# Conv-MoE, attention and dense-MoE block on one core: merge, layer norm, q and k moved into the softmax stage, maxima shifted to the dense layer

## The chip, the core and the metric

One NeuronCore of a Trainium2 chip runs the whole program. The metric is the device time of one execution in microseconds (us); lower is better. The five engines are TensorE (PE), VectorE (DVE), ScalarE (ACT), GpSimd (POOL) and SyncE (SP), which here only issues DMAs.

## What is computed

Eight images of 1024 tokens with 96 channels go through a routed layer, attention and a dense layer. The reference, cut:

```python
# 8 images (32x32x96): E = 8 experts, top 2, hidden 384
logits = gn(x) @ Wg + bg;  gates = softmax(where(top2, logits, -inf))
x = x + sum_e gates_e * (gelu(gn(x) @ W1_e + b1_e) @ W2_e + b2_e)      # routed layer
t = ln(x);  q, k, v = split(t @ w_attn.T + b_attn)                     # 6 heads of 16, T = 1024
att = softmax(causal(q @ k.T / 4));  x = x + (att @ v) @ w_proj.T + b_proj
p = topk2(softmax(ln(x) @ gate_w + gate_b)), renormalised              # 4 experts
x = x + sum_e p_e * (gelu(ln(x) @ w1_e + b1_e) @ w2_e + b2_e)          # dense: all 4 are computed
```

## The kernel before

Only two experts of eight are computed in the first layer: the 2048 token copies of an image are sorted by expert into `NBLK` = 23 blocks of 128 rows, with DRAM between (a scatter of x rows to `xs_dram`, a gather of results from `y_dram`). The second layer computes all four experts. float32 accuracy comes from pairs of float16 values: ScalarE writes a high half from PSUM, VectorE then the low half (`low_part`, L1095, and `xs_turn`, L1281), and only the low half frees the bank. Transposes, gate logits and v share one PSUM bank, `ps_m`, in strict turn (`shared()` on each engine); the next user waits for the last one's release.

The order is written out by hand. A loop over `it` from -1 to 10 runs three stages, and each stage is a row of steps (`steps`, L84 on):

- stage a, 28 steps: the routed layer of image `it`, six groups of four blocks, a group in four steps.
- stage s, 26 steps: the scores, exponentials and value products of image `it-1`. Step n has three heads of one 128-key block. PE does the scores of step n and then the values of step n-2; ScalarE takes exponentials in step n. The maxima of the softmax are subtracted by way of two more rows in `qs`, which `maxima` (L1315 on) fills for three heads at a time.
- stage c, 32 steps: the dense layer of image `it-2`, eight groups.

Beside these, tables name chores: (step, chore, unit, offset of the image). `IN_A`, `IN_S`, `IN_C` serve the regular iterations, special tables serve it -1, 0 and 1. Every engine walks the same steps and does its own part of each chore, in order and without looking ahead. So the place in the table is a place in the queue of each engine, not a time: an engine without a wait runs on. On PE the chores of a step come after its scores and values. On VectorE `max` chores come first in a step.

The chores that matter here:

- `max` (72 an image, `MAX_UNITS`): PE puts q·k of 128 queries and up to 512 keys into one of three `ps_r` banks, VectorE reduces it (L1313). In stage s only two banks are free for it. `MAX_C` and `MAX_A` say how many are done in stage c, up to the end of stage a, and then in stage s.
- `gather` (POOL, L646): 16 indirect DMAs, ygot from y_dram. `scatter` 0 to 3 (POOL, L659): four indirect DMAs each, for the next image.
- `merge` (VectorE, L1286 to L1291): waits for the gathers of its half, multiplies with the gates and adds to x. `ln1`: VectorE makes mean and variance (L1122, L1125), POOL the reciprocal deviation (`rstd`, L625 and L627), `ln1_apply` on VectorE waits for it (L1129, L1133). `x1_turn`: PE waits for `xn1_ready`, transposes (L698), ScalarE high half, VectorE low half. `qk`: three matmuls of 512 columns each, for four units. `stack`: SP takes q and k through DRAM into `qs` and `ks`. `val`: v into `vaug`.
- `prefetch` (SP, L471): one block's weights, 336 KB, from DRAM into the ring `wring` of 16.
- `sums`, `sum_inverse`, `normalise_y`, `project`: the end of attention; `ln2`, `x2_turn`, `logits_c`, `route_c`: before the dense layer.

## Time and profile before

| | us |
|---|---|
| median of 3 runs | 1541.68 (1536.09 to 1546.77) |
| the profiled execution | 1539.89 |
| its span, first to last instruction | 1538.1 |
| PE busy | 1138.4 (74%) |
| DVE busy | 787.7 (51%) |
| ACT busy | 751.5 (49%) |
| POOL busy | 698.1 (45%) |

Matmuls overlap, so a PE that is busy for 74% of the span may have nothing left to give in a stage: what counts is whether it stands still between two matmuls and what it then waits for. Times in the rows are from the start of the span. Stages can be told by the tiles: `ps_u<-xsh,wring` is stage a, `ps_r<-qs,ks` and `probs` stage s, `ps_u<-xch,w1c` stage c. There are eight stages s; seven of them have gathers beside them, six have scatters too, and the last, at 1399.5, has neither.

### The profile page before, as it was taken

What the parts mean: (1) busy time and instruction counts of PE and PEld (TensorE: products, weight loads), DVE (VectorE), ACT (ScalarE), POOL (GpSimd) and SP (SyncE); (2) the same over time, 40 slices, a digit from 0 to 9 for tenths busy, and PEclk for the clock granted to TensorE, in tenths of its full rate; (3) what the DMA queues carried; (4) which work ended last, traced back from release to release, by engine and by line L of the source; (5) the groups of instructions that cost most, each with busy time, mean ns of one, the idle gap of its engine ahead of it and who ended that gap; (6) DMA issues with size and microseconds to landing.
All of it is one profiled execution on the core that took longest, in us unless ns stands there. A gap on an engine that the chain in (4) does not pass through costs nothing.

```text
span 1538.1 us, 30223 instructions
## 1 busy us (share of the span) xinstructions
PE 1138.4 (74%) x11069; PEld 693.7 (45%) x11069; DVE 787.7 (51%) x2278; ACT 751.5 (49%) x1526; POOL 698.1 (45%) x709
## 2 busy tenths in 40 slices
PE   1173367675859887788869894988787987878978
PEld 1163364223723574246723682357524662453355
DVE  6254238334734475427735573547542764376253
ACT  0242342352526753566437752666346654733756
POOL 3353532330643556265545565356526562440257
PEclk9975577785969898899969997999879997986988
DMA  7564350046212721253313631273124330310010
GB/s 174 156 196 143 96 125 24 19 135 137 85 35 87 181 86 45 82 105 94 106 25 116 159 91 41 83 162 109 44 81 97 101 108 11 54 32 1 2 33 12
DMA packets 109873, 133.59 MB, mean 87 GB/s; under 512 B 63542, under 2 KB 72071, under 8 KB 109725
## 3 DMA queue, kind: packets, MB, share of 16 engines
q1 hardware_dynamic: 77213, 110.01, 27.4%
q0 software_dynamic: 8192, 12.60, 3.2%
q10 hardware_dynamic: 24320, 9.05, 2.2%
q8 instruction: 88, 1.44, 0.4%
q14 instruction: 60, 0.49, 0.1%
HBM read 101.23 MB, written 29.98 MB: 85 GB/s over the span
## 4 chain that ended last, share of the span: by engine, by line
PE 40%; DVE 17%; DMA 9%; issue 8%; ACT 7%; another core or an unknown queue 6%; POOL 5%; SPq 4%; DVEq 3%; POOLq 1%; ACTq 0%
PE ps_y L682 14%; PE ps_u L682 11%; PE ps_r L682 10%; DVE mpart L1313 7%; PE ps_m L682 4%; ACT probs L1004 3%; DMA sums<-yt 2%; DMA rb<-rsum_dram 2%; POOL hidl L670 2%; DMA qk_dram<-qk_hl 2%; PE ps_m L698 2%; POOL xs_dram L659 1%; SPq L539 1%; DMA ks<-qk_dram 1%
## 5 line engine op out<-in xcount | busy, mean ns | idle before, releaser
L670 POOL TENSOR_TENSOR hidl<-hid,hidh 128x512 f16<-128x512 f32 x336 | 389.6, 1174 | 428.2 <-ACT hidh L975 427.0
L1313 DVE TENSOR_REDUCE mpart<-ps_r 128x1 f32<-128x512 f32 (+2 forms) x576 | 297.2, 552 | 244.9 <-PE ps_r L682 123.9
L682 PE MATMUL ps_r<-ks,qs 96*128 96x512 f16 (+2 forms) x576 | 204.2, 391 | 171.0 <-DVE mpart L1313 133.1
L974 ACT ACTIVATE hid<-ps_u 128x512 f32<-128x512 f32 x336 | 198.7, 591 | 251.8 <-PE ps_u L682 217.8
L1004 ACT ACTIVATE probs<-ps_r 128x512 f32<-128x512 f32 x192 | 95.1, 495 | 212.9 <-PE ps_r L682 118.2
L975 ACT ACTIVATE hidh<-ps_u 128x512 f16<-128x512 f32 x336 | 198.6, 591 | 0.0
L682 PEld LDWEIGHTS ps_r<-ks,qs 96*128 96x128 f16 x576 | 59.4, 108 | 265.3 <-DVE mpart L1313 178.9
L1004 ACT ACTIVATE probs<-ps_u 128x512 f32<-128x512 f32 (+3 forms) x384 | 169.4, 499 | 19.1 <-remote 13.0
L682 PE MATMUL ps_y<-probs,vaug 128*32 128x512 f32 (+3 forms) x1152 | 176.2, 541 | 0.0
L659 POOL DMA_INDIRECT xs_dram<-xtok,slots x128 | 130.9, 1022 | 76.3 <-DVEq L1173 41.1
L646 POOL DMA_INDIRECT ygot<-y_dram,slots x128 | 121.8, 952 | 80.6 <-issue 41.5
L682 PE MATMUL ps_u<-xch,w1c 97*128 97x512 f16 x384 | 125.9, 412 | 13.2 <-ACT hidh L975 10.6
L682 PE MATMUL ps_u<-xsh,wring 97*128 97x128 f16 x1104 | 122.7, 236 | 5.3 <-DMA wring<-wq_dram 3.5
L682 PE MATMUL ps_u<-qs,ks 98*128 98x512 f16 (+3 forms) x384 | 121.9, 367 | 2.6
L682 PE MATMUL ps_u<-xsl,wring 97*128 97x128 f16 x552 | 113.3, 237 | 0.0
L682 PE MATMUL ps_y<-w2c,hidh 128*128 128x96 f16 x1536 | 110.1, 209 | 0.0
L682 PEld LDWEIGHTS ps_u<-xsh,wring 97*128 97x128 f16 x1104 | 96.7, 108 | 13.7 <-DMA wring<-wq_dram 3.5
L625 POOL TENSOR_TENSOR rstd<-mv,epsilon 128x4 f32<-128x4 f32 x32 | 7.0, 220 | 206.0 <-DVEq L1126 205.2
L682 PE MATMUL ps_r<-mask_q,identb 128*128 128x128 bf16 x384 | 95.7, 252 | 0.0
L682 PEld LDWEIGHTS ps_y<-w2c,hidh 128*128 128x128 f16 x1536 | 83.0, 99 | 16.4 <-issue 2.9
L698 PE MATMUL ps_m<-ident,xs 128*96 128x128 f32 x184 | 37.8, 341 | 68.3 <-DMA xs<-xs_dram 50.1
L1020 ACT ACTIVATE xsf<-ps_m,gshift,grstd 96x512 f32<-96x512 f32 (+1 forms) x48 | 36.3, 755 | 106.6 <-PE ps_m L698 106.0
(206 smaller groups left out, 2110.4 us busy)
## 6 DMA issues: line engine op xcount, KB each, us to landing
wring<-wq_dram SPq DMA_DIRECT2D x184, 336.0 KB, 3.7
y_dram<-ysort ACTq DMA_DIRECT2D x40, 192.0 KB, 2.9
qk_dram<-qk_hl SPq DMA_DIRECT2D x32, 192.0 KB, 2.9
rb<-rsum_dram SPq DMA_DIRECT2D x24, 256.0 KB, 4.3
qs<-qk_dram SPq DMA_DIRECT2D x24, 192.0 KB, 4.9
ks<-qk_dram SPq DMA_DIRECT2D x24, 192.0 KB, 7.6
xtok<-in_x_dram SPq DMA_DIRECT2D x8, 384.0 KB, 6.0
out_dram<-xtok SPq DMA_DIRECT2D x8, 384.0 KB, 3.1
```

Of the source, the lines that this page charges most:

```text
L539: sp.dma_start(sums[n:n + TT, :], yt[32 * g + HD:32 * g + HD + 1, t, :] .rearrange("a (i q) -> a i q", q=P)).then_inc(sums_in, 16)
L625: g.tensor_tensor(dst, var, epsilon[0:rows, 0:cols], ALU.add)
L646: g.indirect_dma_start(out=ygot[:, n, t, :], out_offset=None, in_=y_dram[b % 2], in_offset=bass.IndirectOffsetOnAxis(ap=slots[:, b % 2, n, ...
L659: g.indirect_dma_start(out=xs_dram[b % 2], out_offset=bass.IndirectOffsetOnAxis(ap=slots[:, b % 2, n, t:t + 1], axis=0), in_=xtok[:, b % X ...
L670: g.tensor_tensor(hidl[:, grp.k % 2, s.j, 0:w], hid[:, s.j, 0:w], hidh[:, grp.k % 2, s.j, 0:w], ALU.subtract).then_inc(hl_ready, 1)
L682: return nc.tensor.matmul(dst, lhsT, rhs, start=start, stop=stop, skip_group_check=True)
L698: last = nc.tensor.transpose(ps_m[0:D, P * i:P * (i + 1)], tile, ident[:])
L974: a.activation(hid[:, j, 0:w], bank[:, 0:w], ACT.Gelu, scale=1.0 / WS)
L975: a.activation(hidh[:, grp.k % 2, j, 0:w], bank[:, 0:w], ACT.Gelu, scale=1.0 / WS).then_inc(h_ready, 1)
L1004: a.activation(probs[:, n % 3, g, 0:w], soft_bank(k)[:, 0:w], ACT.Exp, scale=float(HD) ** -0.5).then_inc(p_ready, 1)
L1020: a.activation(xsf[:, k % 2, 0:w], ps_m[0:D, 0:w], ACT.Identity, bias=gshift[:], scale=grstd[:]).then_inc(xsf_ready, 1)
L1313: v.tensor_reduce(mpart[:, h // TR, h % TR, i, part:part + 1], max_bank(k)[:, 0:w], AX, ALU.max).then_inc(mx_free, 1)
```

## The change

Maxima: of the 72 units, 40 instead of 20 are done in stage c, 14 instead of 32 in stage a, 18 instead of 20 in stage s. In stage s everything up to k moves forward: the last steps of `route_c`, `merge` and `ln1` (step 12 to 9, 19 to 14), `ln1_apply` (16 to 11, 23 to 16), `x1_turn` (24 to 12, stage c 0 to stage s 17) and `qk` (stage c 2 to 5, to stage s 18 to 22, now on two banks). `scatter` 0 goes from before the gathers to after the first `ln1`, and `scatter` 1 is now also before the second `ln1`. `stack` and `val` go to the start of stage c. The gather is written as eight chores of two DMAs. Weight fetches are placed earlier and get waits on PE's progress. On VectorE the low halves of `x1_turn`, `x2_turn`, `xs_turn` and `qk` are done a step later than the rest of their chore (`BEHIND`).

```diff
-MAX_C, MAX_A = 20, 52
+MAX_C, MAX_A = 40, 54
+BEHIND = {"x1_turn", "x2_turn", "xs_turn", "qk"}
 IN_A = [(6, "store", 0, -3), (1, "ln2", 0, -2), (2, "ln2", 1, -2),
         (5, "ln2_apply", 0, -2), (7, "ln2_apply", 1, -2), (10, "x2_turn", 0, -2), (12, "x2_turn", 1, -2),
-        (15, "logits_c", 0, -2), *maxima_at(0, 13, MAX_C, HALF_MAX, -1), (14, "maxima", 0, -1),
-        *maxima_at(16, 27, HALF_MAX, MAX_A, -1), *NORM]
-IN_S = [(0, "exp_c", 0, -2), (0, "exp_a", 0, 1), (0, "scatter", 0, 1), *maxima_at(0, 7, MAX_A, MAXU, -1),
-        (8, "maxima", 1, -1), (1, "gather", 0, 0), (1, "gather", 1, 0),
-        (2, "route_c", 0, -2), (9, "route_c", 1, -2), (9, "route_c", 2, -2), (10, "route_c", 3, -2),
-        (12, "merge", 0, 0), (13, "ln1", 0, 0), (14, "scatter", 1, 1), (16, "ln1_apply", 0, 0),
-        (19, "merge", 1, 0), (19, "ln1", 1, 0), (20, "scatter", 2, 1), (20, "scatter", 3, 1),
-        (23, "ln1_apply", 1, 0), (24, "x1_turn", 0, 0), *fetches(range(10, 26, 2))]
-IN_C = [(0, "x1_turn", 1, 0), (2, "xs_load", 0, 1), (2, "gate_a", 0, 1),
-        (2, "qk", 0, 0), (3, "qk", 1, 0), (4, "qk", 2, 0), (5, "qk", 3, 0), (6, "stack", 0, 0), (6, "stack", 1, 0),
-        (7, "val", 0, 0), (9, "val", 1, 0), (8, "sums", 0, -1), (10, "x_load", 0, 2), (13, "sum_inverse", 0, -1),
-        *maxima_at(15, TC * GC - 1, 0, MAX_C, 0), *fetches(range(14, 30, 2), 8),
+        (15, "logits_c", 0, -2), *maxima_at(0, TC * (GA + 1) - 1, MAX_C, MAX_A, -1), *NORM]
+IN_S = [*((n, "gather", n, 0) for n in range(TT)), (0, "exp_c", 0, -2), (0, "exp_a", 0, 1),
+        *maxima_at(0, 6, MAX_A, MAXU, -1), (7, "maxima", 1, -1), *fetches(range(2, 18, 2)),
+        (2, "route_c", 0, -2), (5, "route_c", 1, -2), (7, "route_c", 2, -2), (8, "route_c", 3, -2),
+        (9, "merge", 0, 0), (9, "ln1", 0, 0), (10, "scatter", 0, 1), (11, "ln1_apply", 0, 0), (12, "x1_turn", 0, 0),
+        (12, "scatter", 1, 1), (14, "merge", 1, 0), (14, "ln1", 1, 0), (16, "scatter", 2, 1),
+        (16, "ln1_apply", 1, 0), (17, "x1_turn", 1, 0), (18, "scatter", 3, 1),
+        (18, "qk", 0, 0), (20, "qk", 1, 0), (21, "qk", 2, 0), (22, "qk", 3, 0)]
+IN_C = [(0, "stack", 0, 0), (0, "stack", 1, 0), (1, "val", 0, 0), (3, "val", 1, 0),
+        (4, "xs_load", 0, 1), (4, "gate_a", 0, 1), (6, "sums", 0, -1), (10, "x_load", 0, 2),
+        (11, "sum_inverse", 0, -1), *maxima_at(6, 28, 0, HALF_MAX, 0), (29, "maxima", 0, 0),
+        *maxima_at(30, TC * GC - 1, HALF_MAX, MAX_C, 0), *fetches(range(8, 24, 2), 8),
         (19, "normalise_y", 0, -1), (21, "normalise_y", 1, -1),
@@ qk_bank
-            return ps_r[k % len(ps_r)]
+            return ps_r[1 + k % 2]
@@ SP's walk over the steps
+                        if name == "prefetch" and s.phase == "s" and 0 <= it - 1 < NIMG:
+                            wait(sp, s_full, SU * (it - 1) + TR * s.j)
+                        if name == "prefetch" and s.phase == "c":
+                            wait(sp, up_full, HT * grp.k)
@@ POOL, gather: 8 chores of 2 DMAs for 2 chores of 8
@@ PE, qk: the waits follow the two banks; its wait for p_ready moves to the first max
@@ VectorE's walk over the steps
-                    run_chores(m, chore, sorted(chores(table, it, s), key=lambda c: c[0] != "max"))
+                    now = list(chores(table, it, s))
+                    run_chores(m, chore, [c for c in now if c[0] == "max"])
+                    run_chores(m, chore, behind + [c for c in now if c[0] != "max" and c[0] not in BEHIND])
+                    behind = [c for c in now if c[0] in BEHIND]
```

## Rows read from the trace of the kernel before

**Rows 1.** Stretches: window, length, busy (instructions) by engine, granted clock, DMA share, GB/s.
```profile
888.40:933.20 44.80, 37.42 (x603) 33.47 (x601) 36.01 (x122) 22.82 (x46) 26.09 (x27) 0.96 0.31 89
933.20:997.50 64.30, 47.27 (x302) 16.05 (x303) 26.23 (x91) 31.86 (x76) 27.16 (x30) 0.81 0.23 64
997.50:1053.40 55.90, 46.46 (x484) 31.94 (x482) 28.71 (x64) 37.90 (x69) 34.01 (x29) 0.94 0.57 134
1256.40:1320.10 63.70, 50.97 (x301) 16.56 (x301) 26.25 (x91) 31.30 (x75) 17.79 (x20) 0.79 0.07 15
1399.50:1448.00 48.50, 45.67 (x298) 15.95 (x299) 17.46 (x63) 32.03 (x75) 0.00 (x0) 0.89 0.01 1
```

**Rows 2.** The same view, stretches in which no expert is computed.
```profile
330.40:384.70 54.30, 28.27 (x132) 18.31 (x130) 22.19 (x40) 14.21 (x21) 2.57 (x3) 0.57 0.59 135
1374.00:1399.50 25.50, 15.83 (x80) 6.75 (x81) 21.32 (x55) 1.18 (x2) 2.21 (x3) 0.54 0.06 17
```

**Rows 3.** Timeline of PE, stage s: start, length, instruction, [idle before <- releaser].
```profile
959.00 0.39 PE L682 MATMUL ps_r<-ks,qs 96*128 96x256 f16 x1 [9.55 <-DVE mpart L1313]
```

**Rows 4.** Timeline of POOL, the same stage s: first and last of 16 gathers.
```profile
935.05 0.98 POOL L646 DMA_INDIRECT ygot<-y_dram,slots  x1 [0.30 <-issue]
...
953.86 0.94 POOL L646 DMA_INDIRECT ygot<-y_dram,slots  x1 [0.30 <-issue]
```

**Rows 5.** Timeline of DVE, the same stage s.
```profile
973.19 0.28 DVE L1084 SCALAR_TENSOR_TENSOR mtl<-ps_m,mth 24x128 f16<-24x128 f32 x1
...
974.32 0.09 DVE L1361 MATCH_VALUE_LOAD order_c<-top_c,prob_c 128x8 f32 x1
...
981.09 0.38 DVE L1125 BATCH_NORM_AGGREGATE mv<-st 128x2 f32<-128x6 f32 x4
...
984.64 0.56 DVE L1133 TENSOR_TENSOR xn<-xn,rstd 128x384 f32<-128x384 f32 x1 [1.91 <-POOL rstd L627]
...
986.48 1.01 DVE L1286 TENSOR_TENSOR ygot<-ygot,gate_a 128x384 f32<-128x384 f32 x2
...
989.67 0.38 DVE L1125 BATCH_NORM_AGGREGATE mv<-st 128x2 f32<-128x6 f32 x4
```

**Rows 6.** Timeline of POOL, the same stage s, after the gathers.
```profile
986.44 1.43 POOL L659 DMA_INDIRECT xs_dram<-xtok,slots  x1 [0.30 <-issue]
...
989.44 0.95 POOL L659 DMA_INDIRECT xs_dram<-xtok,slots  x1 [0.31 <-issue]
990.41 0.40 POOL L625 TENSOR_TENSOR rstd<-mv,epsilon 128x4 f32<-128x4 f32 x1
...
993.21 1.30 POOL L659 DMA_INDIRECT xs_dram<-xtok,slots  x1 [0.20 <-issue]
```

**Rows 7.** Timeline of PE, stage s: scores open steps 13, 17, 18; then `x1_turn`.
```profile
978.64 0.34 PE L682 MATMUL ps_r<-qs,ks 98*128 98x384 f16 x1
...
984.28 0.39 PE L682 MATMUL ps_r<-qs,ks 98*128 98x512 f16 x1
...
985.75 0.39 PE L682 MATMUL ps_r<-qs,ks 98*128 98x512 f16 x1
...
996.55 0.64 PE L698 MATMUL ps_m<-ident,xn 128*96 128x128 f32 x4
```

**Rows 8.** Timeline of PE, stage c: two of the 12 matmuls of `qk`.
```profile
1002.74 0.38 PE L682 MATMUL ps_r<-xbh,wqh 97*96 97x512 f16 x1
1002.96 0.38 PE L682 MATMUL ps_r<-xbh,wql 97*96 97x512 f16 x1
```

**Rows 9.** Timelines of DVE and PE, stage c: last low half of k, first maximum.
```profile
1009.98 0.69 DVE L1095 SCALAR_TENSOR_TENSOR qk_hl<-ps_r,qk_hl 96x512 f16<-96x512 f32 x1 [0.77 <-ACT qk_hl L1037]
...
1024.71 0.29 PE L682 MATMUL ps_r<-ks,qs 96*128 96x128 f16 x1 [4.25 <-DMA ks<-qk_dram]
```

**Rows 10.** Stretches, stage c: right behind that first maximum.
```profile
1024.40:1031.20 6.80, 6.49 (x30) 3.69 (x31) 3.57 (x9) 3.21 (x6) 2.31 (x2) 0.50 0.36 79
```

**Rows 11.** Waits in the stage a at 888.4: total, times, longest.
```profile
PE ps_r L682 <- DVE mpart L1313: 2.9, 1, 2.9
```

More of the change, by code:

```diff
@@ L170, in schedule @@
                 *((20 + n, "zero", n, None) for n in range(ZEROS))]
-        in_s = [(1, "exp_a", 0, 1), (0, "gather", 0, 0), (0, "gather", 1, 0)]
+        in_s = [(1, "exp_a", 0, 1), *((0, "gather", n, 0) for n in range(TT))]
         in_c = [(0, "xs_load", 0, 1), (0, "x_load", 0, 2), *fetches(range(1, 17)), *sorted_in(range(2, 2 + GA), 1)]
@@ L175, in schedule @@
                 (5, "merge", 1, -1), (5, "ln1", 1, -1), (6, "ln1_apply", 1, -1), (6, "gate_a", 0, 0),
-                (7, "x1_turn", 0, -1), (9, "x1_turn", 1, -1), (11, "qk", 0, -1), (12, "qk", 1, -1), (13, "qk", 2, -1),
+                (8, "x1_turn", 0, -1), (10, "x1_turn", 1, -1), (11, "qk", 0, -1), (12, "qk", 1, -1), (13, "qk", 2, -1),
                 (14, "qk", 3, -1), (15, "stack", 0, -1), (15, "stack", 1, -1), (16, "val", 0, -1), (18, "val", 1, -1), *((slot + 1, *rest) for slot, *rest in NORM),
@@ L643, in chore @@
                         pool.wait_ge(xs_ready, GA * max(b + 1, 2))
-                    for t in range(TC * k, TC * (k + 1)):
-                        for n in range(TOP):
-                            g.indirect_dma_start(
-                                out=ygot[:, n, t, :], out_offset=None, in_=y_dram[b % 2],
-                                in_offset=bass.IndirectOffsetOnAxis(ap=slots[:, b % 2, n, t:t + 1], axis=0)
-                            ).then_inc(gathered[k], 16)
+                    for n in range(TOP):
+                        g.indirect_dma_start(
+                            out=ygot[:, n, k, :], out_offset=None, in_=y_dram[b % 2],
+                            in_offset=bass.IndirectOffsetOnAxis(ap=slots[:, b % 2, n, k:k + 1], axis=0)
+                        ).then_inc(gathered[k // TC], 16)
                 if name == "scatter":
@@ L806, in qk @@
                 if k == 0:
-                    wait(pe, p_ready, SU * b)
                     wait(pe, mx_free, MAXU * b)
-                wait(pe, qk_free, 2 * NC * b + k - len(ps_r) + 1)
+                wait(pe, qk_free, 2 * NC * b + k - 1)
                 tok = slice(CH * c, CH * (c + 1))
@@ L825, in maximum @@
                     pe.wait_ge(qk_free, 2 * NC * (b + 1))
+                    wait(pe, p_ready, SU * b)
                 wait(pe, mx_free, MAXU * b + max_before[k] + 1)
@@ L1378, in _ @@
             dve.drain().then_inc(xs_zero, 1)
+            behind = []
             ends_of = {TC: 0, TC + 2 * TC: 1, TC + 3 * TC: 2, 2 * (TC + 2 * TC): 3}
```

## The prediction

> **What bounds the kernel now.** I read the table of stretches first, because a mean over 1538 us hides three stages with different limits. One regular iteration is 44.8 us of stage a, 64.3 us of stage s and 55.9 us of stage c [rows 1]. In stages a and c PE stands still for a few us only: in a one wait of 2.9 us is long [rows 11], in c one of 4.25 us, for k to come back from DRAM [rows 9]. So whatever PE does there costs its own time, and a chore moved out gives that back. In stage s PE is busy for 47.3 of 64.3 us. The last stage s, with the same scores and no gathers, takes 48.5 us [rows 1]. The difference, 15.8 us, is one hole: between two maxima PE waits 9.55 us [rows 3] and ScalarE, VectorE wait with it, all while POOL issues gathers, from 935.05 to 954.8 [rows 4]. It ends about 4 us behind the last one. The stage at 1256.4 has gathers and no scatters and is as long, 63.7 us [rows 1]: the gathers belong to the hole, the scatters don't. Behind the hole the stage is full: steps 4 to 25 in 997.5 - 959.0 = 38.5 us, 1.75 a step.
>
> **The hole.** The change writes the gather as eight chores, but POOL has nothing to wait for between them, so they go out in one row as before. Without `scatter` 0 ahead they could start up to 5 us earlier, but the stage at 1256.4, without scatters, had its hole as long. I take 0. Bounds: if the hole went, 15.8 us in each of seven stages (64.3 less 48.5), a gain of 110 us; and two weight fetches (steps 2 and 4) now go out beside the gathers, and if each put off the end of the hole by its 3.7 us to landing (the page's list of DMA issues), 7 x 7.4 = 52 us more. The Trainium skill, page "SBUF — State Buffer", section "Who interferes with whom", says that a DMA never contends with a compute engine and that PE and ACT never wait on anyone. By that the fetches could not lengthen PE's hole, but the gathers could not make it either, and the two stages differ just by them. The rows decide, and the 52 us stay a bound.
>
> **The steps after the hole; here the change costs.** Times are those of the stage at 933.2. Everything up to `maxima` 1 keeps its place, but it is at step 7 and not 8, with 18 units and not 20: VectorE is done with `mtl` at about 971.9 instead of 973.47 [rows 5]. From the start of `order_c` to the end of `mv` it takes 981.47 - 974.32 = 7.15 us; `top_c` was done before. So the first half's variance is ready at 979.0. From there to the end of the scaled `xn` it took 985.20 - 981.47 = 3.7 us, by way of POOL's `rstd` [rows 5]: 982.8. PE, though, reaches `x1_turn` at the end of step 12, just before what was the start of step 13, 978.64 [rows 7]. The two units fewer, the third in step 6 and the earlier transpose cancel. PE waits 4.2 us, and behind it in its queue are the scores of step 13, on which ScalarE and the values wait. Before, x1_turn was at step 24 and waited for nothing. With the transpose itself, 0.6 us [rows 7], step 13 starts at 983.3, 4.7 us late.
>
> The second half is worse. `merge` 1 follows the copy of `yt` in step 13, which needs PE; it starts at about 985.4, and to the variance it takes 990.05 - 986.48 = 3.6 us [rows 5]: 989.0. But POOL's queue now has `scatter` 0 and 1, eight DMAs, between the two `rstd`; before there were four. Alone one takes (953.86 - 935.05) / 15 = 1.25 us from start to start [rows 4], beside merge 1 (989.44 - 986.44) / 2 = 1.5 [rows 6]. The first `rstd` is done 984.64 - 981.47 = 3.1 us behind its variance [rows 5], at 982.1: 982.1 + 4 x 1.25 + 4 x 1.5 = 993.1, where 989.0 would do. Then `rstd`, 993.21 - 990.41 less 0.2 of issue, is 2.6 us [rows 6], the scaling 0.6: 996.3. PE is at `x1_turn` 1 in step 17, which starts 5.6 us after step 13 [rows 7], plus its work of 1.1: 990.0. It waits 6.3 us more. The Trainium skill, same page and section "SBUF: two separate sides", warns that VectorE can lock POOL out while it writes descriptors: 620 ns alone, 3100 ns beside a copy. With 3.1 us for each of the eight the stage would be 14.7 us longer again (an estimate from that page). The row beside merge shows 1.43 at most [rows 6], so the trace doesn't agree.
>
> From step 18, at 996.9, the rest took 997.5 - 985.75 = 11.75 us, with a transpose that is now gone (0.6). Added are the 12 matmuls of qk at 0.22 us [rows 8], 2.65: PE has nothing to hide them behind. After a wait of 4.25 us TensorE's granted clock was 0.50 for 6.8 us, that is 1.2 GHz and not 2.4 [rows 10]; at half clock 6.8 us of work are worth 3.4. Behind the first wait that eats into the second, behind the second I add half, 1.7. The stage ends at 996.9 + 11.75 - 0.6 + 2.65 + 1.7 = 1012.4: 79.2 us for 64.3, +14.9. Six stages have this. The one without scatters has no queue on POOL: +10.3 by the same steps. The last has no merge: 2 units fewer, -1. Sum: 6 x 14.9 + 10.3 - 1 = **+98.7**. Bounds for a stage: +2.7 if the waits don't arise, +18 if both half clocks cost in full.
>
> **Stage a.** 18 maxima go. A unit is at most 512 columns, 0.22 us as in [rows 8]; with the mask about 0.2 on average: -3.7. The 2.9 us wait [rows 11] is on VectorE's backlog of maxima at the end of the stage: it goes, with the half clock behind it, -4.3. The low half of `x2_turn` now waits for the next step on VectorE, and PE's next user of `ps_m` is in that step, twice: +0.5 each. -7.0 x 6 = **-42**. Bounds -3 to -9 a stage.
>
> **Stage c.** 20 maxima more, +4.1; 12 qk matmuls less, -2.65; x1_turn 1 and its small waits less, about -1.5. k comes back 14 us after its last low half (1024.7 - 1010.7) [rows 9]. In the new order that low half falls 1 to 2 us before the end of stage s, and PE is at the first maximum, now at step 6, about 8 us into the stage: it waits 4 to 5 us, as before. Forty reductions of 0.55 us (the page's group of `mpart`, mean 552 ns) are 22 us of VectorE's 28.7 - 10 + 22 = 41 in 50: it hardly keeps up, +1. +1.0 x 6 = **+6**. Bounds -3 to +5. The paced fetches cost nothing: each still lands a whole stage ahead of its block.
>
> **Fill and drain.** With no expert beside it, stage c at 330.4 lasts 54.3 us, PE busy for 28.3 [rows 2]. The last low half of k moves from about 13 us into the stage (1010.7 - 997.5) [rows 9] to just before it, -14; 20 more maxima at 0.6 us (0.55 and the hand-over) are +12, and I take it that about 5 of these fall into waits for the sums, which stay: **-7** (0 to -14). Stage a at 1374.0 holds 32 maxima, 21.3 us of VectorE in 25.5 [rows 2]; 18 fewer at 0.6: **-11** (at most, since `ln2`, `x2_turn` and `logits_c` remain).
>
> Sum: 98.7 - 42 + 6 - 7 - 11 = +44.7. The profiled execution took 1539.9, its span 1538.1 (1.8 around it); the median is 1541.7, 0.1% more, which I leave out. 1539.9 + 44.7 = 1585.
>
> **Rivals.** (1) *The waits at x1_turn don't arise*, because PE reaches steps 12 and 17 more than 4 and 6 us later than I think. Then stage s costs 2.65 of qk, about +3: 8 x 3 - 42 + 6 - 18 = -30, **1510**. For it: all else moved is cheap. Against: VectorE's chain of 7.15 + 3.7 us starts at a point that PE's own maxima set, and PE runs four steps meanwhile. It is the case on the other side, and it decides as soon as the two waits together are under 3 us a stage (6 x 7.4 = 44). (2) *Half of it*: the first wait is there, POOL has its scatters out in time and the second is short; about 7 us less in six stages: **1543**. Against: eight DMAs stand before the second `rstd` in program order. (3) *The hole shrinks* with the order of POOL's queue: with half of it gone in seven stages, -55: **1530**. Against: the stage without scatters. (4) *The hole grows* by the fetches, +26 to +52: **1611 to 1637**. (5) *The change does what it says it does, and VectorE is late in stage c*: PE waits for its banks there, 3 us more in six stages: **1603**.
>
> **Numbers.** My case with (5), slower by 20 to 80 us: 0.60. (4): 0.08. (2): 0.10. (1): 0.12. (3) and other gains in the hole: 0.10. About 1% is what a measurement of this kernel can tell from no change, 1526 to 1557. Slower 0.68, same 0.13 (most of (2), part of (3)), faster 0.19. The range leaves out (1) in full and the upper end of (4): 1528 to 1618. My case alone: 1560 to 1605.
>
> **What would show it.** Right: in stages s two waits of PE for `xn` (DVE L1133 or its queue) at the transposes, 4 and 6 us, eight scatters between the two `rstd` of POOL, stage s 76 to 82 us; the 9.55 us hole at its place; stage a 36 to 39 us, stage c 54 to 60. Wrong: stage s at 67 us or less, or the gathers beside a PE that doesn't stand still.

## The result, and the profile after

In runs side by side on one chip the kernel before took 1543.16 us (median of 4, 1536.09 to 1546.77) and the changed kernel 1580.84 us (median of 4, 1575.65 to 1583.7): ratio 1.0246, 95% interval 1.02 to 1.0292. The profiled execution has a span of 1578.8 us, where that of before had 1538.1: 40.7 us more. The forecast was 1585, from +44.7.

The table of stretches of the changed kernel (window, length, busy us and instructions of PE, PEld, DVE, ACT, POOL, granted clock, DMA share, GB/s). The rows are one regular stage a, s and c, the stage s without scatters and the last one; they answer to [rows 1]:

```profile
911.30:950.90 39.60, 31.84 (x571) 29.58 (x569) 27.54 (x99) 22.55 (x46) 24.25 (x24) 1.00 0.34 98
950.90:1031.80 80.90, 59.98 (x314) 20.16 (x315) 30.18 (x97) 35.31 (x82) 34.27 (x36) 0.73 0.22 61
1031.80:1088.20 56.40, 47.17 (x503) 32.76 (x501) 36.78 (x82) 34.63 (x63) 30.12 (x24) 0.94 0.53 120
1299.10:1370.00 70.90, 54.09 (x318) 18.86 (x316) 29.86 (x96) 35.49 (x82) 17.82 (x20) 0.81 0.08 20
1440.60:1488.30 47.70, 45.51 (x295) 15.63 (x296) 17.21 (x63) 32.05 (x75) 0.00 (x0) 0.89 0.01 1
```

Stage s grew (64.3 to 80.9 here), a shrank (44.8 to 39.6), c stayed (55.9 to 56.4). PE has 12 instructions more in stage s (x314 for x302: 12 of qk, four of the second transpose, four less for two maxima), but 12.7 us more busy time: the clock in that row is 0.73, where before it was 0.81.

One stage is one sample, so I take the five regular stages s together. PE's timeline shows when the scores of each of the 24 steps start; the mean time of groups of steps, in us:

| steps | before | after | difference | the prediction had |
|---|---|---|---|---|
| 0 to 2 | 9.4 | 9.1 | -0.3 | 0 |
| 3 to 7 (the hole) | 27.3 | 27.6 | +0.2 | 0 |
| 8 to 11 | 6.7 | 6.6 | 0.0 | 0 |
| 12 to 14 (first x1_turn) | 4.6 | 10.7 | +6.1 | +4.7 |
| 15 to 18 (second x1_turn) | 6.1 | 13.0 | +6.9 | +6.4 |
| 19 to 22 (most of qk) | 7.0 | 9.7 | +2.6 | +4.4, with the half clock |
| the rest | 2.6 | 1.9 | -0.7 | -0.6, the transpose |
| whole stage | 63.7 | 78.6 | **+14.9** | **+14.9** |

(Differences are taken before rounding. The right column follows from the prediction's start times of steps 13 and 18. One of qk's four chores falls in step 18.)

The stage at 1299.1, which has no scatters, is a control inside the same run: its steps 12 to 14 take 10.7 us like the others', but its steps 15 to 18 only 7.0 instead of 13.0. So the scatters account for 6.0 us of the second wait's 6.9.

What PE waits for in the stage at 950.9, from its timeline (start, length, instruction, [idle before <- releaser]; the first row is the last but one matmul for a maximum before the hole):

```profile
961.23 0.28 PE L688 MATMUL ps_r<-ks,qs 96*128 96x256 f16 x1
...
973.81 0.61 PE L688 MATMUL ps_r<-ks,qs 96*128 96x512 f16 x1 [12.02 <-DVE mpart L1319]
...
1001.51 1.09 PE L704 MATMUL ps_m<-ident,xn 128*96 128x128 f32 x4 [3.35 <-DVEq L1141]
...
1012.06 0.39 PE L688 MATMUL ps_r<-qs,ks 98*128 98x512 f16 x1 [2.06 <-issue]
1013.37 0.88 PE L688 MATMUL ps_u<-qs,ks 98*128 98x512 f16 x2 [0.92 <-ACT probs L1010]
1015.05 1.09 PE L704 MATMUL ps_m<-ident,xn 128*96 128x128 f32 x4 [0.33 <-DVEq L1141]
```

The second row is the hole, at its place as in [rows 3]. The third is the first wait for `xn`. The last is the second `x1_turn`, and it has almost no wait, 0.33. The two rows above it show why: PE is late itself, by waits that the prediction did not have. Here are POOL and then DVE over the same time; POOL's answers to [rows 6], DVE's to [rows 5]:

```profile
998.13 0.20 POOL L632 TENSOR_TENSOR rstd<-mv,epsilon 128x4 f32<-128x4 f32 x1 [25.60 <-DVEq L1132]
999.79 1.04 POOL L634 TENSOR_TENSOR rstd<-rstd,power 128x4 f32<-128x4 f32 x1 [1.46 <-issue]
1001.03 1.32 POOL L665 DMA_INDIRECT xs_dram<-xtok,slots  x1 [0.20 <-issue]
...
1010.63 0.97 POOL L665 DMA_INDIRECT xs_dram<-xtok,slots  x1 [0.30 <-issue]
1011.62 0.21 POOL L632 TENSOR_TENSOR rstd<-mv,epsilon 128x4 f32<-128x4 f32 x1
1013.33 1.04 POOL L634 TENSOR_TENSOR rstd<-rstd,power 128x4 f32<-128x4 f32 x1 [1.49 <-issue]
```

```profile
1000.86 0.56 DVE L1139 TENSOR_TENSOR xn<-xn,rstd 128x384 f32<-128x384 f32 x1 [2.13 <-POOL rstd L634]
...
1014.40 0.56 DVE L1139 TENSOR_TENSOR xn<-xn,rstd 128x384 f32<-128x384 f32 x1 [5.03 <-POOL rstd L634]
```

Eight scatters stand between the two `rstd`, from 1001.03 to 1011.6, and VectorE's second scaling waits 5.03 us for the `rstd` behind them. And the late PE, from the timelines of PE and ACT:

```profile
1008.62 0.39 PE L688 MATMUL ps_r<-qs,ks 98*128 98x512 f16 x1
```

```profile
1007.95 0.44 ACT L1010 ACTIVATE probs<-ps_u 128x128 f32<-128x128 f32 x2
1011.40 0.60 ACT L1010 ACTIVATE probs<-ps_r 128x512 f32<-128x512 f32 x1 [3.02 <-remote]
```

The matmul is over at 1009.01. ScalarE's next exponential needs it and the values of step 13, over at 1008.69, and starts at 1011.40. In a quiet step the same takes 0.3 us (matmul to 1002.91, exponential at 1003.18). The profile writes `remote` where a semaphore was raised and no instruction of the core had ended shortly before. The trace's records of the semaphore that this matmul raises have it at 1011.32, 2.3 us behind the matmul's end and 0.08 before the exponential: ScalarE was not late by itself, PE's completion was, while scatters went out. The hole under the gathers looks the same from inside: the matmul of the first row above is over at 961.51, its semaphore is recorded at 973.30, and VectorE's reduction starts at 973.33, with the releaser `remote` too. (The ends of matmuls are modelled in these profiles. Whether the matmul's result or only its report is late, they don't tell.)

### The profile page after: what moved, and what is told of

It reads as the page before. It is cut to its first block, busy times and chain, and to the rows that moved or that the text cites. A ratio compares the mean times of both kernels' runs of the same rounds, so it can differ in the third digit from the quotient of the medians.

```text
span 1578.8 us, 30224 instructions
## 1 busy us (share of the span) xinstructions
PE 1152.0 (73%) x11069; PEld 696.1 (44%) x11069; DVE 797.2 (50%) x2278; ACT 749.8 (47%) x1526; POOL 710.1 (45%) x709
## 3 DMA queue, kind: packets, MB, share of 16 engines
q0 software_dynamic: 8192, 12.60, 3.1%
## 4 chain that ended last, share of the span: by engine, by line
PE 33%; issue 20%; POOL 15%; DVE 9%; DMA 8%; DVEq 5%; SPq 4%; ACT 4%; POOLq 1%; ACTq 0%; another core or an unknown queue 0%
PE ps_y L688 11%; PE ps_u L688 9%; POOL ygot L652 8%; PE ps_r L688 7%; DVE mpart L1319 4%; DMA ks<-qk_dram 4%; POOL hidl L676 3%; PE ps_m L688 3%; POOL xs_dram L665 2%; PE ps_m L704 2%; DMA qk_dram<-qk_hl 2%; DVEq L1288 2%; POOL rstd L634 1%; ACT hidh L981 1%; DVE xtok L1118 1%
## 5 line engine op out<-in xcount | busy, mean ns | idle before, releaser
L676 POOL TENSOR_TENSOR hidl<-hid,hidh 128x512 f16<-128x512 f32 x336 | 401.1, 1209 | 477.4 <-ACT hidh L981 476.6
L688 PE MATMUL ps_r<-ks,qs 96*128 96x512 f16 (+2 forms) x576 | 200.6, 391 | 157.0 <-DVE mpart L1319 68.8
L688 PE MATMUL ps_y<-probs,vaug 128*32 128x512 f32 (+3 forms) x1152 | 188.0, 577 | 0.0
L688 PE MATMUL ps_u<-qs,ks 98*128 98x512 f16 (+3 forms) x384 | 128.8, 390 | 5.7 <-ACT probs L1010 3.1
L688 PE MATMUL ps_u<-xch,w1c 97*128 97x512 f16 x384 | 121.1, 398 | 6.0 <-ACT hidh L981 4.3
L688 PE MATMUL ps_u<-xsh,wring 97*128 97x128 f16 x1104 | 118.3, 234 | 6.3 <-DMA wring<-wq_dram 3.7
L688 PE MATMUL ps_u<-xsl,wring 97*128 97x128 f16 x552 | 109.9, 234 | 0.0
L688 PE MATMUL ps_r<-qs,ks 98*128 98x512 f16 x192 | 76.5, 398 | 31.3 <-ACT probs L1010 19.5
L688 PEld LDWEIGHTS ps_y<-w2c,hidh 128*128 128x128 f16 x1536 | 84.0, 100 | 14.7 <-issue 0.8
L688 PE MATMUL ps_y<-wring,hidl 128*128 128x96 f16 x552 | 58.7, 220 | 37.5 <-POOL hidl L676 37.1
```

The costliest lines, as they stand in the source:

```text
L676: g.tensor_tensor(hidl[:, grp.k % 2, s.j, 0:w], hid[:, s.j, 0:w], hidh[:, grp.k % 2, s.j, 0:w], ALU.subtract).then_inc(hl_ready, 1)
L688: return nc.tensor.matmul(dst, lhsT, rhs, start=start, stop=stop, skip_group_check=True)
```

## The experiments

Each ratio is to the kernel before, run beside the experiment. Its median was 1534.71 us for e1 to e4, 1538.23 for e5 to e8, 1544.12 for e9 to e11 and 1543.84 for e12, so ratios can be compared between these groups, and times only roughly.

The first four take the change apart.

**e1, the maxima alone.**

```diff
 (kernel before)
-MAX_C, MAX_A = 20, 52
+MAX_C, MAX_A = 40, 54
-        *maxima_at(0, 13, MAX_C, HALF_MAX, -1), (14, "maxima", 0, -1), *maxima_at(16, 27, HALF_MAX, MAX_A, -1)
+        (2, "maxima", 0, -1), *maxima_at(0, TC * (GA + 1) - 1, MAX_C, MAX_A, -1)
-        *maxima_at(0, 7, MAX_A, MAXU, -1), (8, "maxima", 1, -1)
+        *maxima_at(0, 6, MAX_A, MAXU, -1), (7, "maxima", 1, -1)
```

> The kernel before with the shift of the maxima alone: 40 of them in stage c (steps 15 to 31), the transpose of the first half in step 2 of stage a, 14 in stage a, 18 in stage s; merge, layer norm, q and k, the low halves and the fetches as before. My account of the change (each part costs what it costs by itself): stage a 4 to 5 us shorter as in the changed kernel (6 x -4.5 = -27), the drain -8, stage c +4 to +6 for 20 more maxima with q and k still in it (6 x 5 = +30), stage s -0.4 each: about -5, 1530 to 1545. Rival, VectorE is late in stage c: 40 reductions of 0.55 us stand in 17 steps, and if it doesn't keep up there stage c gets another +3 each: 1555 to 1565.

Measured: 1600.28 us, ratio 1.0412 (1.0352 to 1.0473). Worse than the whole change, and worse than the rival. Mean stage c went from 57.5 to 68.8 us, stage s from 63.7 to 67.1, stage a from 45.8 to 42.6. The stretch of one stage c:

```profile
1042.00:1111.30 69.30, 56.15 (x519) 36.58 (x517) 38.82 (x84) 38.96 (x69) 33.38 (x28) 0.85 0.47 107
```

PE's waits there sum to 13.1 us (9.3 in the stage c at 997.5 of before), 6.4 of them for VectorE's reductions (0.8), and its busy time is 9.7 us more for 20 maxima and a lower clock (0.85 for 0.94). The first maximum still comes only when k is back, in the middle of the stage, and twice as many are crowded behind it. The shift of the maxima is no gain by itself; it needs q and k early. The 3.4 us more in stage s are all in the hole (steps 3 to 7 take 31.5 us for 27.3; the steps behind it are as before). The gathers start 4.5 us into the stage instead of 1.8; whether that lengthens the hole wasn't tried. So the hole isn't a fixed cost, though it stayed the same from before to after.

**e2, the chain alone.**

```diff
 (changed kernel)
-MAX_C, MAX_A = 40, 54
+MAX_C, MAX_A = 20, 52
 and the maxima of stages a, s and c in the steps of the kernel before
```

> The changed kernel with the maxima back in their old places (20, 52; transposes in step 14 of stage a and step 8 of stage s; those of stage c from step 15): the moved chain of merge, layer norm, x1_turn, q and k is left, with the low halves and the paced fetches. If the chain is what costs, stages s are 77 to 82 us as in the changed kernel, stage a is back at 45 to 47, stage c gives 3 to 4 us back for q and k: 6 x 15 + 7 - 6 x 3 = +79, about 1610 to 1630. Rival, the cost comes from the interplay of the chain with the earlier maxima (18 units and not 20, so that PE arrives earlier at x1_turn than the variance): then stage s is 70 us or less here and the time below 1580.

Measured: 1592.01 us, ratio 1.0399 (1.0329 to 1.0469). Its stages s, c and a:

```profile
968.00:1045.20 77.20, 55.51 (x318) 19.72 (x319) 30.26 (x97) 35.22 (x82) 33.88 (x36) 0.78 0.22 63
1045.20:1094.70 49.50, 43.08 (x469) 30.06 (x467) 26.04 (x58) 34.33 (x63) 28.89 (x24) 0.93 0.59 137
1094.70:1142.80 48.10, 38.78 (x604) 34.27 (x602) 36.20 (x122) 22.82 (x46) 23.39 (x24) 0.93 0.29 83
```

Mean stage s is 78.7, the same as in the changed kernel (78.6): the whole +15 of stage s is there without the shift of the maxima, and the rival that wanted the interplay is out. The rest comes out by difference. Moving q, k and the transposes out of stage c gives, together with the paced fetches and the later low halves that this kernel keeps, 57.5 - 50.4 = 7.1 us, and 20 more maxima take back 56.9 - 50.4 = 6.5. In stage a the fewer maxima give 48.0 - 41.0 = 7.0, and before that something had cost 48.0 - 45.8 = 2.2. By spans, e1 is +62.3, e2 is +49.4, and both together +40.7: the two parts are worth 71 us more together than one by one. (These are spans of single executions on two chips. The ratios say it more surely: 1.0412 and 1.0399 against 1.0246, with intervals that don't meet.)

**e3, the scatters behind the second `ln1`.**

```diff
 (changed kernel)
-(10, "scatter", 0, 1), ... (12, "scatter", 1, 1), (14, "merge", 1, 0), (14, "ln1", 1, 0),
+(14, "merge", 1, 0), (14, "ln1", 1, 0), (14, "scatter", 0, 1), (14, "scatter", 1, 1),
```

> The changed kernel with the first two scatter chores (8 DMAs) behind the second ln1 in POOL's queue; nothing else. By the queue theory the second scaling of xn no longer waits 5.03 us for POOL's rstd, the second x1_turn no longer meets a late PE or a late xn, and a stage s is 4 to 6 us shorter in six stages: 1545 to 1558. Rival: beside the scatters it is PE's own completions that arrive late (2.06 and 0.92 us in steps 16 and 17), and PE, not POOL, sets the time there; then the late completions move on to the steps after 17 with the scatters and the stage is at most 2 us shorter: 1567 to 1580.

Measured: 1613.39 us, ratio 1.0521 (1.0462 to 1.058): slower, which neither theory had. Steps 15 to 18 fell from 13.0 to 7.1 us, so POOL's queue did cost its 6 us there. But steps 19 to 22 rose from 9.7 to 18.2, and the rest of the stage from 1.9 to 4.8. From the timelines of PE and POOL:

```profile
1228.71 0.63 PE L688 MATMUL ps_r<-xbl,wqh 97*96 97x512 f16 x1
1234.70 0.29 PE L688 MATMUL ps_r<-qs,ks 98*128 98x128 f16 x1 [5.35 <-ACT probs L1010]
```

```profile
1211.33 1.33 POOL L665 DMA_INDIRECT xs_dram<-xtok,slots  x1 [0.19 <-issue]
...
1230.67 0.96 POOL L665 DMA_INDIRECT xs_dram<-xtok,slots  x1 [0.30 <-issue]
```

Sixteen scatters now stand in one row of 20 us. Up to 1222, ten us into it, PE works without a stop. Then it waits 0.53, 0.63 and 1.75 us, works from 1225.5 to 1229.3, and stands until 3.1 us behind the last DMA (1230.67 + 0.96 to 1234.70). That is the shape of the hole, made by scatters and over 40 us behind the last gather (it ended at 1176.7). In the stage without scatters steps 19 to 22 and the rest take 9.2 and 1.9 us as ever. So it is a matter of sixteen indirect DMAs in a row, not of the gathers.

**e4, the fetches in their old steps, unpaced.**

```diff
 (changed kernel)
-*fetches(range(2, 18, 2))      and in stage c   -*fetches(range(8, 24, 2), 8)
+*fetches(range(10, 26, 2))                      +*fetches(range(14, 30, 2), 8)
-                        if name == "prefetch" and s.phase == "s" and ...: wait(sp, s_full, ...)
-                        if name == "prefetch" and s.phase == "c": wait(sp, up_full, HT * grp.k)
```

> The changed kernel with the weight fetches in their old steps (10 to 24 of stage s, 14 to 28 of stage c) and without the waits that pace them. By my forecast the fetches cost nothing: within 4 us of the changed kernel. Rival, the fetches beside the gathers lengthen PE's stop in steps 3 and 4 (10.3 to 12.0 us after, 8.3 to 9.5 before): the stop goes back by 2 to 3 us in seven stages, 1560 to 1567.

Measured: 1583.38 us, ratio 1.0326 (1.0267 to 1.0384); its interval and that of the changed kernel (1.02 to 1.0292) overlap, so the whole is not told from no difference. Inside, both theories have a part: mean stage s is 76.0 instead of 78.6 (steps 3 to 7: 25.7 for 27.6), stage c 58.6 instead of 56.9, stage a 40.1 instead of 41.0. The fetches beside the gathers do cost 2 us of hole a stage, and the paced ones give most of it back in stage c.

The next four test the hole, the low halves and the first wait.

**e5, the gathers not in one row.**

```diff
 (kernel before)
-(1, "gather", 0, 0), (1, "gather", 1, 0)            # eight DMAs each
+*((s, "gather", n, 0) for n, s in enumerate((1, 3, 5, 7, 9, 11, 12, 13)))      # two DMAs each
 (POOL's loop)
+                        if name == "gather" and s.phase == "s" and s.j and 0 <= it - 1 < NIMG:
+                            pool.wait_ge(s_full, SU * (it - 1) + TR * s.j)
```

> The kernel before, its 16 gathers no longer in one row: pairs in steps 1, 3, 5, 7, 9, 11, 12 and 13 of stage s, each pair waiting for the scores of the step before. What is known: sixteen indirect DMAs in a row (gathers in steps 0 to 4, or scatters from step 14 when all stood behind ln1) bring one stop of 9 to 14 us near their end, eight of them 2 to 3 us, four none. Theory 1, PE's completions pile up only behind a long row: with gaps the stop of steps 3 and 4 is gone, at most 3 us of small waits come for it, 8 to 12 us less in seven stages: 1450 to 1485. Theory 2, each indirect DMA holds PE's completions back by the same amount wherever it stands: the stop is spread over the steps, the stage stays 62 to 65 us: 1525 to 1545.

Measured: 1482.97 us, ratio 0.9637 (0.959 to 0.9684). Theory 1 holds: the same 16 gathers, and steps 3 to 7 take 12.6 us instead of 27.3. One stage s:

```profile
898.80:953.80 55.00, 48.02 (x302) 16.24 (x302) 26.29 (x91) 31.52 (x75) 26.68 (x29) 0.88 0.26 75
```

What is left is one stop, 3.08 us of PE's wait before step 13, where four gathers stand in a row and two more close on either side; steps 12 to 14 take 9.8 us instead of 4.6.

**e6, plain DMAs for the gathers.**

```diff
 (kernel before)
-                            g.indirect_dma_start(out=ygot[:, n, t, :], out_offset=None, in_=y_dram[b % 2],
-                                in_offset=bass.IndirectOffsetOnAxis(ap=slots[:, b % 2, n, t:t + 1], axis=0)
+                            rows = P * (TOP * t + n)
+                            g.dma_start(out=ygot[:, n, t, :], in_=y_dram[b % 2][rows:rows + P, :]
                             ).then_inc(gathered[k], 16)
```

> The kernel before with each gather replaced by a plain DMA of the same bytes (128 rows of 384 bytes from consecutive places of the same DRAM tensor), issued by POOL at the same place: the indices are left out, so the wrong rows of the routed layer's output are added. If the stop in steps 3 and 4 comes from what POOL does for an indirect DMA (0.94 us busy, 1.25 from start to start), it goes: stage s near 50 us, 7 x 13 = -90, about 1450. If it comes from the data landing (2048 packets of 384 bytes in the tile), it stays or is shorter only as the transfers are: 1500 to 1540.

This kernel leaves out the indices, so it adds rows of other tokens and doesn't compute the function; only its time is of use. Measured: 1424.87 us, ratio 0.9267 (0.9202 to 0.9332). Stage s is 49.0 us, about the length of the last stage of before (48.5), and its steps 3 to 7 take 12.5 us, as they do there: the hole is gone altogether. The page's group for these DMAs:

```profile
L647 POOL DMA_DIRECT2D ygot<-y_dram x128 | 68.6, 565 | 44.1 <-DVEq L1281 26.1
```

The packets (8192 in POOL's queue), their size and where they land are as before, so it isn't the landing. But POOL needs 0.565 us for each instead of 0.952, and the row of 16 is over in 8.6 us instead of 20. Whether a plain DMA is harmless or only a short row, this run doesn't tell.

**e7, the low halves back in their own step.**

```diff
 (changed kernel)
-BEHIND = {"x1_turn", "x2_turn", "xs_turn", "qk"}
+BEHIND = set()
```

> The changed kernel with VectorE's low halves back in their own step. My forecast gave the later low half +0.5 us for each x2_turn of stage a, nothing elsewhere: six stages 1 us shorter, 1575, not to be told from 0. Rival, the low halves behind the next step's maxima keep VectorE from stopping at ScalarE's copies, and are part of what shortened stages a and c: without that stage a gets 2 to 3 us longer and stage s and c 1 to 2: 1600 to 1615.

Measured: 1575.19 us, ratio 1.024 (1.0187 to 1.0293), the same as the changed kernel within its interval. By stages: a 38.9 instead of 41.0, c 57.9 instead of 56.9, s 77.9 instead of 78.6. So the later low halves cost the 2.2 us of stage a that e2 had left open. They give 1.0 back in c.

**e8, the first `x1_turn` two steps later.**

```diff
 (changed kernel)
-(11, "ln1_apply", 0, 0), (12, "x1_turn", 0, 0),
+(11, "ln1_apply", 0, 0), (14, "x1_turn", 0, 0),
```

> The changed kernel with the first x1_turn in step 14 instead of 12; VectorE's and POOL's order stays but for the low half, one step behind it. By my account PE stands 3.3 to 4.2 us at this transpose for the variance's chain, and the score steps 13 and 14 (1.5 and 1.4 us plus values) cover most of it: 3 to 4 us less in seven stages, 1553 to 1562. Rival, the gain goes into the next wait: PE comes earlier to steps 16 and 17, where POOL's eight scatters and the second rstd set the time, and the second wait grows by what the first one loses: 1574 to 1584.

Measured: 1570.64 us, ratio 1.0221 (1.0167 to 1.0276): the rival, all but a rest. Steps 12 to 14 fell from 10.7 to 5.6 us, and steps 15 to 18 rose from 13.0 to 18.6; stage s is 77.7 us, 0.8 shorter. PE and POOL in the stage at 947.6:

```profile
1010.66 1.09 PE L704 MATMUL ps_m<-ident,xn 128*96 128x128 f32 x4 [9.31 <-DVEq L1141]
```

```profile
1006.25 0.97 POOL L665 DMA_INDIRECT xs_dram<-xtok,slots  x1 [0.30 <-issue]
1007.23 0.22 POOL L632 TENSOR_TENSOR rstd<-mv,epsilon 128x4 f32<-128x4 f32 x1
1008.94 1.04 POOL L634 TENSOR_TENSOR rstd<-rstd,power 128x4 f32<-128x4 f32 x1 [1.49 <-issue]
```

PE comes earlier and waits 9.31 us for the second `xn`. Into the stage, POOL's second `rstd` is done at 1009.98 - 947.6 = 62.4 us, in the changed kernel at 1014.37 - 950.9 = 63.5. It is POOL's row, first `rstd`, eight scatters, second `rstd`, that sets the time of the second `x1_turn`; the first wait stands in its shadow and costs next to nothing of its own. The stage without scatters is not set by POOL's row, and yet it gains no more, 70.0 for 70.9: steps 12 to 14 fall from 10.7 to 5.3 us, and steps 15 to 18 rise from 7.0 to 11.5, for a second wait of 1.94 us and the slower matmuls behind it. So there, too, the two waits trade places, for a reason that I only have in part.

The last four put the findings together.

**e9, gathers and scatters spread, on the kernel before.** As e5, with the gathers in steps 1, 3, 5, 7, 9, 11, 13, 15 and

```diff
-(14, "scatter", 1, 1), ... (20, "scatter", 2, 1), (20, "scatter", 3, 1),
+(17, "scatter", 1, 1), ... (20, "scatter", 2, 1), (22, "scatter", 3, 1),
-                        if name == "gather" and s.phase == "s" and ...
+                        if name in ("gather", "scatter") and s.phase == "s" and ...
```

> The kernel before with pairs of gathers in steps 1, 3, 5 to 15 and the later scatters of four in steps 17, 20 and 22, each waiting for the scores of its step. e5 left one stop, 3.3 us in step 12, where its last six gathers and four scatters stood in one row. If it is the length of the row that counts, this stop goes as well and a stage s is 50 to 51 us instead of 54.4: 6 x 3.5 = 21 us less than e5, about 1462. If the number of indirect DMAs in the stage counts, the stop moves behind step 17 and the time stays at 1480.

Measured: 1465.36 us, ratio 0.9492 (0.944 to 0.9545), the fastest kernel here that computes everything. Stage s is 50.4 us:

```profile
894.10:944.10 50.00, 45.65 (x301) 15.51 (x301) 26.38 (x91) 31.65 (x76) 24.14 (x26) 0.93 0.27 79
```

No long stop is left (PE's longest wait in this stage is 1.1 us), with 32 indirect DMAs in or near the stage as ever. Stage c rose from 58.4 (e5) to 61.4: the last scatters now reach into it, and in the stage c at 944.1 PE waits 4.3 us for POOL's `hidl` behind them, a wait that e5 does not have there.

**e10, the changed kernel with the rows cut.**

```diff
 (changed kernel, with the waits of e9)
-*((n, "gather", n, 0) for n in range(TT))
+*((s, "gather", n, 0) for n, s in enumerate((1, 2, 4, 5, 6, 7, 8, 9)))
-scatters in steps 10, 12, 16, 18 of stage s, xs_load in step 4 of stage c
+scatters in steps 12, 16, 20 of stage s and 1 of stage c, xs_load in step 6 of stage c
```

> The changed kernel with the long rows cut: pairs of gathers in steps 1, 2 and 4 to 9, scatters of four in steps 12, 16, 20 and in step 1 of stage c, all paced by the scores; the load of the sorted tokens goes from step 4 to step 6 of stage c. The chain of merge, layer norm, x1_turn, q and k stays in stage s. If the stop of steps 3 and 4 is a matter of the row, it shrinks though the gathers stand close (20 us of POOL in 23): stage s 58 to 66 us, 1460 to 1510. If at this density the completions pile up all the same, stage s is still over 74: 1560 to 1580. In both cases the first wait at x1_turn, 3 to 4 us, stays.

Measured: 1474.73 us, ratio 0.9549 (0.9496 to 0.9603). Stages s, c and a of one iteration:

```profile
894.40:958.20 63.80, 53.24 (x314) 18.96 (x314) 30.33 (x97) 34.88 (x82) 30.32 (x32) 0.84 0.26 74
958.20:1013.90 55.70, 46.92 (x504) 32.94 (x501) 35.79 (x82) 34.63 (x63) 33.47 (x28) 0.94 0.53 125
1013.90:1054.20 40.30, 31.92 (x572) 29.66 (x572) 27.56 (x99) 22.55 (x46) 24.23 (x24) 1.00 0.33 97
```

Mean stage s is 60.9 instead of 78.6, with steps 3 to 7 at 15.3 and steps 15 to 18 at 7.8. The first wait stays, 3.13 us in this stage, as expected. Stages a and c keep what the change gave them. Beside e9 it is 10.5 us longer in s and 5 to 6 shorter in a and c each. The two aren't told apart: the intervals overlap.

**e11, the changed kernel with plain DMAs for the gathers**, the edit of e6, with the indices left out as there.

> The changed kernel with plain DMAs of the same bytes for the gathers, as in e6 (the indices are left out): the change without the long stop. My account of the other terms says that they don't need the stop: the first wait 4, the second with the eight scatters 5 to 6, q and k and half clock 4, less two units, so stage s is 13 to 15 us longer than the 49 of e6 and the whole time 1424.9 + 40 = 1460 to 1475. Rival, part of the cost was the end of the stop, half clock in the steps after it and a late chain: then the difference between e11 and e6 is under 20 us, 1430 to 1445.

Measured: 1462.12 us, ratio 0.9486 (0.942 to 0.9552); 37.2 us above e6. Stage s is 63.0 us against 49.0 in e6, +14.0, where with the hole it was +14.9. So the change costs nearly the same with the hole and without it.

**e12, both.**

```diff
 (changed kernel, with the waits of e9)
+gathers in steps 0, 1, 2, 3, 5, 6, 7, 9; scatters in steps 12, 16, 19, 22; xs_turns of stage c one step later
-(12, "x1_turn", 0, 0), ... (17, "x1_turn", 1, 0)
+(14, "x1_turn", 0, 0), ... (18, "x1_turn", 1, 0)
```

> The changed kernel with what the other runs point to: gathers in pairs in steps 0, 1, 2, 3, 5, 6, 7 and 9, scatters in steps 12, 16, 19 and 22, all paced by the scores; the x1_turns in steps 14 and 18 instead of 12 and 17, so that PE comes to them after xn is there; the xs_turns of stage c one step later. If both causes are understood (long rows of indirect DMAs, and PE arriving too early at x1_turn), stage s is the 48 of the stage without a merge plus 2.7 for q and k and 1 to 2 of small waits, stage a stays near 41, stage c near 57: 8 x 4 = 32 to 50 us less than the 1465 of e9: 1415 to 1440. If gathers this close still make the completions pile up in steps 5 and 6, or the twelve scatters in a row stop PE in step 22 by 3 to 6 us, it is 1445 to 1475.

Measured: 1503.89 us, ratio 0.9745 (0.9688 to 0.9801). A miss. POOL starts the first pair 1.8 us into the stage, because the last `ysort` has to be in DRAM, and by then PE's scores are ahead of the waits of steps 1 to 3: the first eight gathers were one row again, 912.41 to 922.2, and step 3 took 5.3 to 5.7 us, where in e11 it took 2.7 to 3.3. The scatters of steps 16 and 19 made another row of eight, and step 18 took 6.5 to 7.3 us, where in the same kernel's stage without scatters it took 5.0. A wait on the step paces nothing when the waiting engine is behind.

## Why the prediction came out

**The hole, 0.** Right as a term: +0.2 us. The prediction read from the stage without scatters that the gathers belong to the hole, and that much is right. What it couldn't read is that sixteen in a row make it and sixteen spread out don't (e3, e5, e9). Its bound of 110 us for a hole that goes was near: e6 is 113 us faster than its kernel before, e9 79. The bound above, 52 us for fetches beside the gathers, had a true core of 2 us a stage (e4). One reading was of a single stage: that the hole ends about 4 us behind the last gather is so in two of the six stages of before with experts beside them; in the other four PE goes on 1.2 to 2.0 us ahead of the row's end, and steps 3 to 7 still take 27.3 us on average.

**The first wait, 4.2 us.** PE waits 3.35 us in the stage shown, and steps 12 to 14 are 6.1 us longer, the rest being the transpose and the clock behind it (granted 0.54 from 1001.5 to 1008.0, where the steps of before had 1.00). But it could not be saved by itself: e8 took it away and the stage got 0.8 us shorter. In the sum of the prediction this was already so, since step 18 was reckoned from POOL's queue (996.3) and not from the first wait. The sentence on rival (1), by which the two waits together decide, said it wrong for the six stages with scatters: there the later of the two chains does.

**The second wait, 6.3 us.** The place and the size of POOL's queue were right: eight scatters between the two `rstd`, VectorE's wait 5.03 us. The prediction had the second `x1_turn` done at 996.9 - 933.2 = 63.7 us into the stage; it was 1016.14 - 950.9 = 65.2. Two things show the term by itself: without the eight scatters in front, steps 15 to 18 are 5.9 us shorter (e3), and in the stage without scatters they are 6.0 shorter. What failed is the sign to look for: no 6 us wait of PE for `xn` but 0.33, because PE's own completions came late beside the scatters (2.06 and 0.92 us) and hid POOL's delay. Two causes stood side by side, and the sum needed only one. The comparison with 3.1 us a DMA in that paragraph tests nothing: the 1.43 us row stands beside tensor-tensor operations of `merge` and not beside a copy, and eight times 3.1 for the sum's 11.0 would be 13.8 us more, not 14.7.

**q and k, +2.65, and half clock, +1.7.** Steps 19 to 22 are 2.6 us longer. The half clock sits earlier, behind each stop: in the stage at 950.9 the granted clock is 0.50 from 973.8 to 990.0 and 0.54 from 1001.5 to 1008.0, and 1.00 from 1025.0 on. At the lower level a score matmul of 512 columns takes 0.63 us, at the upper 0.39.

**Stage s, +14.9 x 6 and +10.3.** Measured +14.9 on average of the five regular ones. The sixth that I gave it is the first, in the fill, which has other work beside it: +7.4. The stage without scatters is 70.9 instead of 63.8, +7.1: three less than I gave it. The 10.3 doesn't come out of the steps given, either: with the second `xn` at 989.0 + 2.6 + 0.6 = 992.2 instead of 996.3 they give 10.8. Measured are +6.1 in steps 12 to 14, +0.9 in 15 to 18, +2.1 in 19 to 22 and -0.8 in the hole: there was no second wait there, and no half clock behind it.

**Stage a, -7.0 a stage.** Measured 45.8 to 41.0, -4.8, outside the 36 to 39 that was to show the forecast right. The maxima were well sized (e2: 7.0 us for the 18 and the wait on VectorE's backlog, 8.0 predicted). Mis-sized is the later low half: +1.0 predicted, 2.2 and 2.1 measured (e2, e7).

**Stage c, +1.0 a stage.** Measured 57.5 to 56.9, -0.6. The maxima cost 6.5 (5.1 predicted, with VectorE's lateness). Of the 7.1 us that e2 gives back, the paced fetches are 1.7 (e4) and the later low halves 1.0 (e7), which leaves 4.4 for q, k and the transposes (4.15 predicted), if these parts add up. What the prediction missed is those two, which it had put at nothing in stage c. The first maximum of the stage at 1031.8 waited 4.5 us for k, as predicted.

**Fill and drain, -7 and -11.** The stage c of the fill went from 54.3 to 50.0 us, -4.3, and the last stage c with the drain from 79.4 to 70.6, -8.8. Not predicted at all: the first stretch, up to the first stage s, is 4.9 us shorter. It is 5 to 6 us shorter in e2, e4, e7 and e8 as well and not in e1, but only 1.2 to 1.4 in e10 and e12, which have the chain too. The cause stays open.

The sum, from the spans: five stages s +74.2, the one without scatters +7.1, the last -0.8, and the first, in the fill, only +7.4: +87.9 for +98.7. Six stages a -26.5 for -42. Five stages c -3.1 for +6. Fill and drain -13.1 for -18. First stretch -4.9 and the stretch behind the last stage s +0.4, both for 0. Together +40.7 for +44.7. So the single terms were off by -10.8, +15.5, -9.1, +4.9, -4.9 and +0.4, and mostly cancelled. The sign rests on stage s, which was well founded; that the total came within 5 us is partly luck.

**The rivals.** (1), no waits: out, by steps 12 to 18 (13.0 us longer). (2), half of it: out, +14.9 and not +7. (3), the hole shrinks: not here; it took e5 to do it. (4), it grows by the fetches: 2 us a stage, most of it given back. (5), VectorE late in stage c: not in the change (PE's waits for reductions sum to 2.5 us in the stage at 1031.8); it is part of what happened in e1.

## What to carry over

Count every DMA that POOL issues between two small results on its queue: eight of them were worth 6 us to whoever waited for the second. And when a stage stands still under a row of indirect DMAs, cut the row before moving work about: pairs paced by the steps of PE took 79 us off the kernel before, twice what the change had cost, while the same number still went out. Two halves of a change have to be tried apart and together; here each alone was worse than both.

## What the runs showed of the hardware

Under a long row of indirect DMAs issued by POOL the completions of matmuls reach the other engines late (2.3 us under a row of eight, 11.8 under sixteen, in the two places shown above), and PE, ScalarE and VectorE come to a stand. The longest stop ended 4.2 us behind the row's last DMA in the stage at 933.2 of before, 1.3 in the one at 950.9 after and 3.1 in e3, but 5 to 6 us ahead of it in e4, with shorter waits behind. What a row cost, each against the same steps without it:

| row | where | cost |
|---|---|---|
| 16 gathers, 20 us | changed kernel, steps 3 to 7, against e11 | 27.6 - 12.0 = 15.6 us |
| 16 scatters, 20 us | e3, step 19 to the end of the stage, against its stage without scatters | 22.9 - 11.0 = 11.9 us |
| 8 scatters, 10 us | changed kernel, steps 19 to 22, against its stage without scatters | 9.7 - 9.2 = 0.5 us |
| 8 and 6 gathers, 10 and 8 us | e12, steps 3 to 7, against e11 | 19.8 - 12.0 = 7.8 us |
| 4, 2, 6, 2, 2 gathers | e10, steps 3 to 7, against e11 | 15.4 - 12.0 = 3.4 us |
| pairs, 2 to 4 us apart | e9, steps 3 to 7, against e6 | 12.5 - 12.5 = 0 |
| 4 gathers in a row, pairs close on either side | e5, steps 12 to 14, against e6 | 9.8 - 4.6 = 5.2 us |
| 2 gathers and 4 scatters, 8 us | e9, steps 18 to 22, against e6 | 9.2 - 9.1 = 0 |
| 16 plain DMAs, 8.6 us | e6, steps 3 to 7, against the last stage of before | 12.5 - 12.5 = 0 |

The sixteen cost much more than twice the eight scatters. But it isn't the row alone: six indirect DMAs cost nothing in steps 18 to 22 of e9, and a shorter row cost 5.2 us in steps 12 to 14 of e5. What makes that difference wasn't tried. The Trainium skill, page "SBUF — State Buffer", section "Who interferes with whom", says that a DMA never contends with a compute engine. The lengths of the instructions agree: at full clock a score matmul of 512 columns takes 0.39 us beside an indirect DMA and away from one, and ScalarE's exponential of 512 columns 0.60 us. The completions that came late don't follow from it. What in the chip holds them back no run here shows, and whether a plain row of 20 us would do the same wasn't tried.
